# Attention probabilities turned by the vector engine and by transfers within SBUF, in place of the tensor engine

## The chip, the core and the metric

The kernel runs on one core of a Trainium2 chip. The metric is the device time of one execution in microseconds (us); lower is better.

The engines are named as in the profile: PE is TensorE (PEld its weight loads), DVE VectorE, ACT ScalarE, POOL GpSimd, SP SyncE, whose queue (SPq) here issues every DMA of the program.

## What is computed

Cross-attention with low-rank additions to the weights, in float32, for 8 batches of 256 queries and 256 context rows of width 1024, with 32 query heads and 8 key/value heads of 32 columns:

```python
q = _lora_linear(hidden_states, Wq, Aq, Bq)      # (8, 256, 1024), 32 heads
k = _lora_linear(traces, Wk, Ak, Bk)             # (8, 256, 256), 8 heads, each used by 4 query heads
v = _lora_linear(traces, Wv, Av, Bv)
scores = einsum('bhqd,bhtd->bhqt', q, k) / sqrt(32)
attn = softmax(scores, axis=-1)
context = einsum('bhqt,bhtd->bhqd', attn, v)
return hidden_states + _lora_linear(context, Wo, Ao, Bo)
```

## The kernel before

A prologue folds the low-rank products into the weights (`fold_mms`) and projects batch 0. Then a loop runs over seven batches (`Fori(0, NB - 1)` on each engine), the last batch is written out after it, and the output projection follows for all batches (`out_batch`).

Every projection operand is split into a high and a low part, so a product is three matmuls. A projection group is 24 matmuls of 256 columns (`group_step`, L858), and a batch has 12 groups (`BODY`).

A batch is 32 **slots**. A slot m works on two heads for 128 queries; four slots make a **unit**, one key/value head with its four query heads. In slot s, each engine does this, in the order written:

- PE (`slot`, L952): `turn` (L893) transposes the probabilities of slot s, four 128x128 transposes through the identity into a PSUM bank; `scores` (L878) makes the scores of slot s + 4, two matmuls; then 9 matmuls of the projection groups (L868). In the first slot of each unit it adds `context` (L901) of the unit before: 8 float32 matmuls, each 128 rows by 32 columns of stationary data with 256 moving columns.
- DVE: copies the turned block from PSUM to `probs_t` in three slots of four (L263), takes the row maxima for slot s + 4 (`row_max`, L718), the reciprocals (L750), evicts the low part of a projection (L712), and copies the context to `ctx_stage` once a unit (L764). The low part of x is made at L725.
- ACT: copies the turned block in the fourth slot (L263), and computes the exponentials (L582), after the turn of slot s has been made, because the buffer `probs` holds four slots.
- POOL: multiplies the probabilities by the reciprocals (`normalize`, L525), 3 slots ahead.

SP is a queue that is worked in order. Projected q and k parts go to DRAM (`send_q`, L305, `send_k`, L310) and come back as three DMAs each (`stack_q`, L293, `stack_k`, L315), in the layout that the scores matmul wants. `wait` (L268) waits for a semaphore before the DMAs that stand behind it, and nothing behind a wait is issued before it ends. The list of one batch is written out by hand in `body` (L362): 4 + 4 input loads, 8 times `stack_q` (24 DMAs), 8 `send_q`, 2 `send_k`, 2 `stack_k` (6 DMAs) and 8 `store_ctx` (L369), 56 DMAs in all.

Of the kernel before, what the change touches and what calls it, by code (L numbers as in the profile page):

```python
# [27 lines left out]
P = 128  # L28
NB = 8
S = 256  # L30
# [12 lines left out]
FIRST = 3  # L43
GROUP_MM = 3 * KT
FILL = 9
DMA = 16
# [11 lines left out]
BODY = [("q", 4, 0), ("q", 5, 0), ("k", 0, 1), ("q", 6, 0), ("q", 7, 0), ("k", 1, 1),  # L58
# [13 lines left out]
V1_EARLY, V1_SLOT = 16, 4  # L72
# [3 lines left out]
def xattn(nc, xt, ct, xn, wq, wkv, wo, a4, b4kv, b4q, b4o, out):  # L76
    with ExitStack() as ctx:
# [18 lines left out]
        v_sb = sb("v_sb", [P, 2, KV], F32)  # L96
        probs = sb("probs", [P, 4, 2, S], F32)
        probs_t = sb("probs_t", [P, 2, 2, GH, S], F32)
# [7 lines left out]
        w_sum = sb("w_sum", [P, 2, 512], F32)  # L106


        probs_flat = probs[:].rearrange("p a b c -> p (a b c)")
        pt_flat = probs_t[:].rearrange("p a b c d -> p (a b c d)")  # L110
# [19 lines left out]
        turn_bank = [banks[:, 4 + i, :] for i in range(2)]  # L130
# [46 lines left out]
        pt_dve = sem("pt_dve")  # L177
        pt_act = sem("pt_act")
# [16 lines left out]
        def end_slot(i):  # L195

            return FIRST + (GROUP_MM * (i + 1) - 1) // FILL

# [50 lines left out]
        def fold_chunks(s):  # L249

            early = (16, 17, 19, 20, 21, 23, 24, 25)
# [4 lines left out]
        def turn_of(unit, c):  # L256

            return turn_bank[(5 * unit + (0, 2, 3, 4)[c]) % 2]

        def copy_turned(op, unit, c):  # L260
            dst = probs_t[:, unit % 2, :, 2 * (c % 2):2 * (c % 2) + 2, P * (c // 2):P * (c // 2 + 1)]
            src = turn_of(unit, c).rearrange("p (t h q) -> p t h q", t=2, h=2)
            return op(dst, src, ACT.Copy) if op == nc.scalar.activation else op(dst, src)  # L263


        @block.sync
        def _(sp):
# [41 lines left out]

            def send_k(m, count):  # L310
# [42 lines left out]
            for g in range(4):  # L353
# [3 lines left out]
            stack_q(2, 2, 4)  # L357

# [3 lines left out]
            def body(b, last):  # L362
# [16 lines left out]

                pos = {g: i for i, g in enumerate(LAST if last else BODY)}  # L380
                for j in range(4):
# [8 lines left out]
                stack_q(3, fills + 2, score0 + 8)  # L390
                store_ctx(0)
                send(pos["q", 4, 0])
                stack_q(4, fills + 3, score0 + 12)
                send(pos["q", 5, 0])
                store_ctx(1)
                for j in range(4):
                    wait(c_ready, b * 4 + (j + 5))
                    if not last:
                        load_inputs(xt, b + 1, j)
                    else:  # L400
                        load_w(FOLD_O + j)
                stack_q(5, fills + 3, score0 + 16)
                if not last:
                    send(pos["k", 0, 1])
                    stack_k(0, b + 2, score0 + 16)
                store_ctx(2)
                send(pos["q", 6, 0])
                stack_q(6, fills + 4, score0 + 20)
                if last:
                    send(pos["q", 7, 0])  # L410

                    for g, loads in ((3, 2), (None, 2), (4, 1), (5, 3), (6, 2), (7, 2)):
                        for _ in range(loads):
                            load_w(next(late_w))
                        if g is None:
                            stack_q(7, fills + 4, score0 + 24)
                        else:
                            store_ctx(g)
                        if g == 6:
                            wait(ctx_mm, NB * NG - 1)  # L420
                            for i in range(2):
                                wait(ctx_stored[i], DMA * (1 + 2 * NG // 2))
                            load_ctx(1, 1)
# [661 lines left out]
```

## Time and profile before

| | |
|---|---|
| time, median of 3 runs (lowest to highest) | 756.04 us (756.01 to 756.3) |
| span of the profiled execution, first to last instruction | 753.1 us |
| granted TensorE clock, mean | 0.998 |
| PE busy | 737.6 us, 98% of the span |
| weight loads busy | 645.2 us, 86% |
| DVE busy | 469.0 us, 62% |
| ACT busy | 382.0 us, 51% |
| POOL busy | 349.1 us, 46% |
| DMA moved | 117.01 MB, mean 155 GB/s |

The profile is of one execution. Its instructions span 753.1 us; the 2.9 us up to the median lie before the first and after the last of them. The busy time of PE comes from modelled ends of pipelined matmuls, so it tells when PE had work and not how fast it was. Issuing a DMA is not counted as busy time of any engine; the issues are rows of SPq in the timeline.

### The profile page before, as it was taken

Reading aid. Unit: us, or ns where it says so; the run is one execution under the profiler, and the core shown is the slowest. Engines: PE = TensorE matmul, PEld = TensorE weight load, DVE = VectorE, ACT = ScalarE, POOL = GpSimd, SP = SyncE. Lnnn points to the kernel's source line nnn. Section 1 sums busy time; section 2 is a strip of 40 time slices with the busy share of each in tenths; the row PEclk is TensorE's granted clock in tenths of the full one; section 3 lists DMA queues with packets and bytes.
Section 4 is the critical chain, followed back from the end, with each engine's and each line's share of the span. In section 5 each row is a group of like instructions: output and inputs, shape, how many; then the busy total and the mean of one; then the engine's idle time right before and its main releaser. Section 6 shows DMA issues by size and latency. Waiting matters only on the chain.

```text
span 753.1 us, 17856 instructions
## 1 busy us (share of the span) xinstructions
PE 737.6 (98%) x5776; PEld 645.2 (86%) x5776; DVE 469.0 (62%) x988; ACT 382.0 (51%) x1287; POOL 349.1 (46%) x322
## 2 busy tenths in 40 slices
PE   7899999999999999999999999999999999999998
PEld 6678899889989989999998998999867788888886
DVE  5957687687768668767876866787696412212211
ACT  4437665666666666666666666665685210111100
POOL 4757645745654574565557457555766100000000
PEclk9999999999999999999999999999999999999999
DMA  7775544554453555345454544645464834343331
GB/s 257 271 219 164 169 140 140 159 172 122 139 174 126 157 152 163 119 139 175 138 156 149 155 131 128 172 139 178 139 181 154 276 130 156 117 167 111 111 111 56
DMA packets 94665, 117.01 MB, mean 155 GB/s; under 512 B 8624, under 2 KB 76208, under 8 KB 94640
## 3 DMA queue, kind: packets, MB, share of 16 engines
q1 hardware_dynamic: 94640, 116.69, 49.3%
q8 instruction: 14, 0.23, 0.1%
q14 instruction: 11, 0.09, 0.0%
HBM read 78.91 MB, written 37.75 MB: 155 GB/s over the span
## 4 chain that ended last, share of the span: by engine, by line
PE 88%; DVE 5%; DMA 2%; issue 2%; POOL 1%; ACT 0%; SPq 0%; POOLq 0%; DVEq 0%
PE banks L868 32%; PE banks L917 23%; PE banks L897 15%; PE banks L906 8%; PE banks L882 7%; DVE neg_max L718 2%; PE banks L853 2%; DVE x_lo L725 2%; DMA probs_t<-wq 1%; PE banks L855 1%; DMA probs<-b4q 1%; DMA probs_t<-b4kv 1%; POOL k_stack L510 1%; DVE lora L679 0%; DVE probs_t L263 0%
## 5 line engine op out<-in xcount | busy, mean ns | idle before, releaser
L525 POOL TENSOR_TENSOR probs<-probs,rsums 128x512 f32<-128x512 f32 x256 | 266.4, 1041 | 205.4 <-DVE rsums L750 204.6
L582 ACT ACTIVATE probs<-banks,neg_max 128x256 f32<-128x256 f32 x512 | 238.7, 475 | 175.7 <-DVE neg_max L718 170.8
L718 DVE TENSOR_REDUCE neg_max<-banks 128x2 f32<-128x512 f32 x256 | 174.3, 682 | 20.0 <-PE banks L882 20.0
L897 PE MATMUL banks<-ident,probs 128*128 128x128 f32 x1024 | 157.1, 276 | 2.2 <-POOL probs L525 2.0
L263 DVE COPY probs_t<-banks 128x512 f32<-128x512 f32 x192 | 132.4, 690 | 43.0 <-PE banks L897 35.6
L868 PE MATMUL banks<-x_hi,w_hi 128*128 128x256 f32 x512 | 145.7, 285 | 0.8 <-POOL w_lo L500 0.4
L868 PE MATMUL banks<-x_hi,w_lo 128*128 128x256 f32 x512 | 144.6, 282 | 0.0
L868 PE MATMUL banks<-x_lo,w_hi 128*128 128x256 f32 x512 | 144.5, 282 | 0.0
L897 PEld LDWEIGHTS banks<-ident,probs 128*128 128x128 f32 x1024 | 115.5, 140 | 30.8 <-issue 27.1
L882 PE MATMUL banks<-k_stack,q_stack 96*128 96x256 f32 x512 | 122.8, 322 | 0.0
L582 ACT ACTIVATION_READ_ACCUMULATOR probs<-banks,neg_max 128x1 f32 x512 | 104.0, 203 | 0.0
L868 PEld LDWEIGHTS banks<-x_hi,w_hi 128*128 128x128 f32 x512 | 97.2, 190 | 2.2 <-DVE x_lo L725 1.6
L868 PEld LDWEIGHTS banks<-x_lo,w_hi 128*128 128x128 f32 x512 | 98.0, 191 | 0.0
L868 PEld LDWEIGHTS banks<-x_hi,w_lo 128*128 128x128 f32 x512 | 97.8, 191 | 0.0
L819 DVE TENSOR_TENSOR raw<-banks,probs 128x512 f32<-128x512 f32 x32 | 21.4, 689 | 118.4 <-PE banks L917 116.7
L882 PEld LDWEIGHTS banks<-k_stack,q_stack 96*128 96x128 f32 x512 | 77.1, 191 | 0.3 <-DMA q_stack<-q_parts 0.3
L906 PE MATMUL banks<-probs_t,v_sb 128*32 128x256 f32 x1024 | 68.5, 385 | 0.0
L764 DVE COPY ctx_stage<-banks 128x256 f32<-128x256 f32 x64 | 27.1, 424 | 55.5 <-PE banks L906 55.5
L917 PE MATMUL banks<-w_hi,c_hi 128*128 128x512 f32 x128 | 49.9, 390 | 0.5 <-POOL w_lo L500 0.5
L917 PE MATMUL banks<-w_lo,c_hi 128*128 128x512 f32 x128 | 49.9, 390 | 0.0
L917 PE MATMUL banks<-w_hi,c_lo 128*128 128x512 f32 x128 | 49.8, 389 | 0.0
L917 PE MATMUL banks<-w_hi,x_hi 128*128 128x512 f32 x128 | 49.8, 389 | 0.0
(76 smaller groups left out, 1112.9 us busy)
## 6 DMA issues: line engine op xcount, KB each, us to landing
q_stack<-q_parts SPq DMA_DIRECT2D x192, 128.0 KB, 2.5
q_parts<-q_stage SPq DMA_DIRECT2D x64, 256.0 KB, 2.2
raw<-ct SPq DMA_DIRECT2D x32, 256.0 KB, 3.9
raw<-xt SPq DMA_DIRECT2D x32, 256.0 KB, 4.4
context<-ctx_stage SPq DMA_DIRECT2D x64, 128.0 KB, 1.8
probs<-xn SPq DMA_DIRECT2D x16, 512.0 KB, 4.1
out<-raw SPq DMA_DIRECT2D x15, 512.0 KB, 2.9
probs_t<-context SPq DMA_DIRECT2D x7, 1024.0 KB, 5.9
```

What stands on the lines that cost most here:

```text
L263: return op(dst, src, ACT.Copy) if op == nc.scalar.activation else op(dst, src)
L525: nc.gpsimd.tensor_tensor(probs[:, c], probs[:, c], rsums[:, c, :].unsqueeze(2).broadcast_to([P, 2, S]), ALU.mult).then_inc(norm_done, 1)
L582: last = nc.scalar.activation(probs[:, c, h, :], score_bank[c][:, S * h:S * (h + 1)], ACT.Exp, bias=neg_max[:, c, h:h + 1], scale=-1.0, ac ...
L718: nc.vector.tensor_reduce(out=neg_max[:, c, :], in_=score_bank[c].rearrange("p (h t) -> p h t", h=2), axis=AXIS, op=ALU.min).then_inc(max_ ...
L725: nc.vector.tensor_tensor(cols[1], raw[:, j, :], cols[0], ALU.subtract).then_inc(ready, 1)
L764: nc.vector.tensor_copy(ctx_stage[:, u % 2, :], turn_bank[(5 * unit + 1) % 2][:, 0:S]).then_inc(ctx_done, 1)
L819: nc.vector.tensor_tensor(out_rows[h][:, cols], banks[:, 4 * i + 2 * h + half, :], x_rows[h][:, cols], ALU.add).then_inc(o_out, 1)
L868: mm = nc.tensor.matmul(proj_bank[bank][:, 0:S], lhs, rhs, start=(k == 0), stop=(k == GROUP_MM - 1))
L882: last = nc.tensor.matmul(score_bank[c][:, S * h:S * (h + 1)], q_stack[0:3 * HD, g % 2, head, P * qh:P * (qh + 1)], k_stack[0:3 * HD, g, : ...
L897: last = nc.tensor.transpose(bank[:, P * (2 * t + h):P * (2 * t + h + 1)], probs[:, c, h, P * t:P * (t + 1)], ident[:])
L906: last = nc.tensor.matmul(bank[HD * h:HD * (h + 1), 0:S], v_sb[:, t, HD * (unit % NG):HD * (unit % NG + 1)], probs_t[:, unit % 2, t, h, :] ...
L917: mm = nc.tensor.matmul(banks[:, 4 * i + 2 * qh + half, :], o_parts[i][t_part][:, kt, P * qh:P * (qh + 1)], w_hl[w_part][:, kt, 512 * half ...
```

## The change

The transposes on PE go. DVE turns the probabilities in blocks of 32x32, SBUF to SBUF, once a slot, into a new tile `turned_in`. Such a turn leaves the context rows spread over the wrong groups of 32 partitions, so that for each unit SP issues 8 DMAs of 32 partitions by 1024 float32 (128 KB each) from `turned_in` to `probs_t`. The copies from PSUM to `probs_t` on DVE and ACT go. The context matmul is cut into 64x32 tiles with 128 moving columns, 32 matmuls in place of 8, over two PSUM banks, and runs two units behind (`LAG = 8` slots) where it ran one slot behind its unit. The v parts are written as two half copies, and two DMAs a batch duplicate them into the other half of the partitions.

With this, FIRST (where the projection groups start in a batch) goes from slot 3 to 5, the order of groups changes (q6 and q7 ahead of k0), two projection groups of the prologue move into its first slots, and `w_sum` shares the memory of `q_stage`.

```diff
+        def turned_out(unit, c):
+            return turned_in[:, unit % 2, :, :, c].rearrange("p e k h q -> p h k e q")
...
+            def move_turned(b, unit, ctxs):
+                wait(turned, b * SLOTS + 4 * unit + 4)
+                if ctxs is not None:
+                    wait(ctx_mm, ctxs)
+                i = unit % 2
+                for half in range(2):
+                    for f in range(2):
+                        for e in range(2):
+                            row, to = 64 * half + 32 * f, 64 * half + 32 * e
+                            sp.dma_start(probs_t[to:to + 32, i, f],
+                                         turned_in[row:row + 32, i, e]).then_inc(pt_moved[i], DMA)
+
+            def copy_v(evicted):
+                wait(proj_out, evicted)
+                for half in range(2):
+                    tiles = v_rep[:].rearrange("p (m k) n -> p k m n", k=2)[:, half]
+                    sp.dma_start(tiles[64 * (1 - half):64 * (2 - half)],
+                                 tiles[64 * half:64 * (half + 1)]).then_inc(v_moved, DMA)
...
+            def turn(n, i, reuse):
+                dve.wait_ge(norm_done, n + (i + 1))
+                if reuse is not None:
+                    dve.wait_ge(pt_moved[(i // 4) % 2], reuse)
+                nc.vector.transpose(turned_out(i // 4, i % 4),
+                                    probs[:, i % 4].rearrange("p h t -> p (h t)")).then_inc(turned, 1)
...
+            def context(b, unit):
+                pe.wait_ge(pt_moved[unit % 2], (b * 4 + (unit // 2 + 1)) * (DMA * MOVES))
+                if unit == 0:
+                    pe.wait_ge(v_moved, b * (2 * DMA) + 2 * DMA)
+                else:
+                    pe.wait_ge(ctx_done, b * NG + unit)
+                pe.sem_inc(pe_waits, 1)
+                for k in range(4):
                     for h in range(GH):
...
+                        for half in range(2):
+                            rows = slice(64 * half, 64 * (half + 1))
+                            moving = probs_t[rows, unit % 2].rearrange("p f k (a c) h q -> p k c h a f q", a=2)
+                            last = nc.tensor.matmul(
+                                ctx_bank[half][HD * h:HD * (h + 1), 0:P],
+                                v_rep[rows, k, HD * unit:HD * (unit + 1)], moving[:, k, h // 2, h % 2],
+                                start=(k == 0), stop=(k == 3), tile_position=(64 * half, HD * h))
```

The list of SP in a batch of the loop becomes: `copy_v`, 4 loads, stack q3, **move 1**, send q4, store 0, stack q4, **move 2**, send q5, 2 loads, store 1, stack q5, send q6, 2 loads, **move 3**, stack q6, store 2, send q7, **move 4**, stack q7, store 3, send k0, **move 5**, stack k0, send k1, send q0, store 4, stack q0, **move 6**, send q1, store 5, stack q1, stack k1, send q2, **move 7**, stack q2, send q3, store 6, **move 0** of the next batch, store 7. (k and q from k0 on are those of the next batch.)

On SP, where the second half of a batch begins. L307 and L310 store q, L312 and L336 store k, L299 and L302 stack q, L320 and L344 stack k, L371 and L397 store the context. Before:

```order
L307 DMA q_parts<-q_stage 128x2x256 [waits proj_out]
L271 REGISTER_ALU [waits q_stored1]
L299 DMA q_stack<-q_parts 32x4x256 [waits scores_mm]
L299 DMA q_stack<-q_parts 32x4x256 x2
L271 REGISTER_ALU
L312 DMA k_parts<-k_stage 128x2x256 [waits proj_out]
L271 REGISTER_ALU
L371 ISA [waits ctx_done]
L371 DMA context<-ctx_stage 128x256
```

and now:

```order
L323 DMA probs_t<-turned_in 32x1024 [waits turned,ctx_mm]
L323 DMA probs_t<-turned_in 32x1024 x7
L274 REGISTER_ALU [waits q_stored1]
L302 DMA q_stack<-q_parts 32x4x256 [waits scores_mm]
L302 DMA q_stack<-q_parts 32x4x256 x2
L274 REGISTER_ALU
L397 ISA [waits ctx_done]
L397 DMA context<-ctx_stage 128x256
L274 REGISTER_ALU
L336 DMA k_parts<-k_stage 128x2x256 [waits proj_out]
```

Eight DMAs more stand in the queue for each unit, between a q store and the stacking of its parts. A batch has 122 DMAs now, 64 of them moves and 2 for v.

On PE, at the first slot of a unit, where the context is made. Before:

```order
L868 MATMUL banks<-x_hi,w_lo 128x256
L1010 REGISTER_ALU
L906 MATMUL banks<-probs_t,v_sb 32x256 [waits pt_dve,pt_act]
L906 MATMUL banks<-probs_t,v_sb 32x256 x7
L956 REGISTER_ALU
L960 REGISTER_ALU [waits norm_done]
L897 MATMUL banks<-ident,probs 128x128 [waits pt_dve]
L897 MATMUL banks<-ident,probs 128x128 x3
L882 MATMUL banks<-k_stack,q_stack 128x256 x2
```

and now:

```order
L957 ISA
L959 REGISTER_ALU [waits pt_moved0]
L968 MATMUL banks<-probs_t,v_rep 32x128 [waits v_moved]
L968 MATMUL banks<-probs_t,v_rep 32x128 x31
L951 ISA
L1026 REGISTER_ALU [waits q_stacked1]
L944 MATMUL banks<-k_stack,q_stack 128x256 [waits exp_done]
L944 MATMUL banks<-k_stack,q_stack 128x256
L930 MATMUL banks<-x_hi,w_hi 128x256
```

The four transposes of the slot are gone, the context has four times as many matmuls, and it waits for the moves' landing.

On DVE, one slot in the middle of a batch. Before:

```order
L263 COPY probs_t<-banks 128x2x2x128 [waits turned]
L717 REGISTER_ALU
L718 TENSOR_REDUCE neg_max<-banks 128x2 [waits scores_mm]
L750 RECIPROCAL rsums<-sums 128x2 [waits exp_done]
```

and now, in the first slot of a unit:

```order
L806 ISA [waits norm_done]
L807 STREAM_TRANSPOSE turned_in<-probs 128x2x4x2x32 [waits pt_moved0]
L767 REGISTER_ALU
L768 TENSOR_REDUCE neg_max<-banks 128x2 [waits scores_mm]
L800 RECIPROCAL rsums<-sums 128x2 [waits exp_done]
```

The transpose takes the place of the copy and stands in every slot; it waits for the normalized probabilities, and once a unit for the moves that read the buffer it writes.

## Rows read from the trace of the kernel before

**Rows 1.** The page: busy time of PE, and the chain that ended last by engine

```profile
PE 737.6 (98%) x5776; PEld 645.2 (86%) x5776; DVE 469.0 (62%) x988; ACT 382.0 (51%) x1287; POOL 349.1 (46%) x322
...
PE 88%; DVE 5%; DMA 2%; issue 2%; POOL 1%; ACT 0%; SPq 0%; POOLq 0%; DVEq 0%
```

**Rows 2.** Stretches: their length; busy us of each engine; clock, DMA share, GB/s

```profile
0.00:20.00 20.00, 15.28 (x84) 14.10 (x85) 10.71 (x13) 8.21 (x13) 9.11 (x12) 0.91 0.77 267
98.00:163.50 65.50, 65.47 (x610) 59.50 (x610) 48.56 (x113) 42.37 (x155) 38.20 (x36) 1.00 0.50 154
523.00:586.00 63.00, 61.97 (x474) 47.91 (x472) 46.53 (x103) 42.71 (x137) 42.97 (x39) 1.00 0.53 161
586.00:753.00 167.00, 163.48 (x720) 135.06 (x720) 37.77 (x40) 12.18 (x7) 0.23 (x1) 1.00 0.40 139
```

**Rows 3.** The chain in order of time: the same step in two batches

```profile
164.38 1.17 DVE x_lo L725
...
229.93 1.17 DVE x_lo L725
```

**Rows 4.** Timeline of PE, a slot and a context: start us, us, engine, line

```profile
303.91 0.60 PE L897 MATMUL banks<-ident,probs 128*128 128x128 f32 x4
304.27 0.48 PE L882 MATMUL banks<-k_stack,q_stack 96*128 96x256 f32 x2
304.58 0.28 PE L868 MATMUL banks<-x_hi,w_hi 128*128 128x256 f32 x1
...
305.55 0.28 PE L868 MATMUL banks<-x_hi,w_lo 128*128 128x256 f32 x1
305.75 1.07 PE L906 MATMUL banks<-probs_t,v_sb 128*32 128x256 f32 x16
306.76 0.33 PE L897 MATMUL banks<-ident,probs 128*128 128x128 f32 x1
```

**Rows 5.** Timeline of SP's queue where it hardly waits, 276 to 293 us

```profile
276.28 0.38 SPq L307 DMA_DIRECT2D q_parts<-q_stage  x1
276.99 0.37 SPq L371 DMA_DIRECT2D context<-ctx_stage  x1
277.60 2.07 SPq L277 DMA_DIRECT2D raw<-xt  x4
279.93 1.28 SPq L299 DMA_DIRECT2D q_stack<-q_parts  x3
281.39 0.38 SPq L312 DMA_DIRECT2D k_parts<-k_stage  x1
```

**Rows 6.** The three DMAs of one stack_q there, one by one

```profile
279.93 0.33 SPq L299 DMA_DIRECT2D q_stack<-q_parts  x1
...
280.31 0.42 SPq L299 DMA_DIRECT2D q_stack<-q_parts  x1
...
280.78 0.43 SPq L299 DMA_DIRECT2D q_stack<-q_parts  x1
```

**Rows 7.** Waits of SP's queue: us in total, times, longest us

```profile
SPq L273 <- DMA q_parts<-q_stage: 60.4, 35, 1.9
```

**Rows 8.** Line L299: issue durations, ns min/median/max, first and last start

```profile
L299 SPq DMA_DIRECT2D q_stack<-q_parts x192: 303/424/1172, 51.2 to 557.9; - x192
```

**Rows 9.** DMA issues: KB each, median us to landing

```profile
q_stack<-q_parts SPq DMA_DIRECT2D x192, 128.0 KB, 2.5
q_parts<-q_stage SPq DMA_DIRECT2D x64, 256.0 KB, 2.2
...
context<-ctx_stage SPq DMA_DIRECT2D x64, 128.0 KB, 1.8
```

**Rows 10.** Groups of DVE instructions: busy us, mean ns; and one timeline row

```profile
L263 DVE COPY probs_t<-banks 128x512 f32<-128x512 f32 x192 | 132.4, 690 | 43.0 <-PE banks L897 35.6
...
L725 DVE TENSOR_TENSOR x_lo<-raw,x_hi 128x512 fp32r<-128x512 f32 x32 | 26.3, 830 | 0.0
...
228.66 0.68 DVE L725 TENSOR_TENSOR x_lo<-raw,x_hi 128x512 fp32r<-128x512 f32 x1
```

More of the change, by code:

```diff
@@ L42 @@
 NORM_AHEAD = 3
-FIRST = 3
+FIRST = 5
 GROUP_MM = 3 * KT
 FILL = 9
+LAG = 8
 DMA = 16
@@ L352, in _ @@
                 stack_k(m, 1, None)
-            for g in range(4):
+            for g in range(3):
                 send_q(g, g + PRO_Q + 1)
@@ L390, in body @@
                 stack_q(3, fills + 2, score0 + 8)
+                move_turned(b, 1, None)
+                send(pos["q", 4, 0])
                 store_ctx(0)
-                send(pos["q", 4, 0])
                 stack_q(4, fills + 3, score0 + 12)
+                move_turned(b, 2, unit0 + 1)
                 send(pos["q", 5, 0])
+                load_x(0)
+                load_x(1)
                 store_ctx(1)
[L396 to L401, printed above, removed]
@@ L409, in body @@
                 if last:
[L410 to L423, printed above, removed]
+                    load_w(next(late_w))
@@ new lines, in body @@
+                    load_w(next(late_w))
+                    load_w(next(late_w))
+                    store_ctx(5)
+                    load_w(next(late_w))
+                    move_turned(b, 7, unit0 + 6)
+                    load_w(next(late_w))
+                    load_w(next(late_w))
+                    store_ctx(6)
+                    wait(pt_moved[0], DMA * MOVES * NB * NG // 2)
+                    for i in range(2):
+                        wait(ctx_stored[i], DMA * (1 + 2 * NG // 2))
@@ L452, in _ @@
                 load_rows(0, h)
-            wait(ctx_mm, NB * NG)
+            wait(pt_moved[1], DMA * MOVES * NB * NG // 2)
             load_ctx(2, 0)
@@ L608, in _ @@
                     high(c_hl, 2 + f, c_hi_done, 1)
-            for g in range(4):
+            for g in range(3):
                 if g == 2:
@@ L637, in slot @@
                         w_high(f)
-                if not prologue and s in (4, 5):
-                    for j in (2 * (s - 4), 2 * (s - 4) + 1):
+                if prologue and s == 3:
+                    proj_high("q", 3, (3 + PRO_Q) % 2, 3 + PRO_Q, DMA)
+                if not prologue and s in (6, 7):
+                    for j in (2 * (s - 6), 2 * (s - 6) + 1):
                         act.wait_ge(proj_mm, b * PER + PRO)
@@ L743, in _ @@
                     proj_low("v", 0, 0, PRO_Q - 1, None, None)
-            for g in range(4):
+            for g in range(3):
                 if g == 2:
@@ L798, in _ @@
                     slot(b, s, False)
-            for s in range(FIRST, SLOTS + 2):
+            for s in range(FIRST, SLOTS + LAG - 3):
                 slot(NB - 1, s, True)
@@ L950, in _ @@
                     group_step(kind, i, j % 2, k)
+            stacks_ready(0, 0)
+            for m in range(4):
+                scores(m, 0, m)
             def slot(b, s, last, prologue=False):
```

185 lines of the change are left out of this document (98 added, 87 removed).

## The prediction

> **What bounds the kernel now.** I read the page first: PE is busy for 98% of the span, and the chain that ended last runs through PE for 88% of it [rows 1]. The stretches say where [rows 2]: a batch of the loop (65.5 us) keeps PE busy for 65.47 us at full granted clock (2.4 GHz), with DVE at 48.56, ACT at 42.37, POOL at 38.20 us and the DMA engines at a share of 0.50. The same step of the chain returns after 229.93 - 164.38 = 65.55 us [rows 3], which I take as the period of a batch; seven batches run so. The last batch takes some 63 us, the output projection 167 us [rows 2], and that one the change leaves alone.
>
> The timeline of PE shows what the period is made of [rows 4]. A slot starts at 303.91 with the transposes, at 304.27 come the scores, at 304.58 the nine projection matmuls. So four transposes cost 0.36 us of PE and two scores 0.31 us. Nine projection matmuls take 1.09 us: the last starts at 305.55 and takes 0.12 like the others' distance, to 305.67. The context then lasts until the next transposes at 306.76, 1.09 us. A unit is 4 x 1.75 + 1.09 = 8.1 us, eight make 65 us: PE fills the period by itself.
>
> The busy table has no row for SP, so its queue has to be read from the timeline [rows 5]. There the queue hardly waits, and the distance from start to start is what each thing costs it, waits and registers included: a load 0.58 us (four in 279.93 - 277.60), a stack of three DMAs 1.46 us, a q store 0.71 us ahead of a context store and about 0.56 otherwise, a context store 0.61. Within a stack the DMAs start 0.38 and then 0.47 us apart [rows 6]. For a batch: 8 loads 4.7 us, 10 stacks 15 us, 10 q and k stores 6 us, 8 context stores 4.8 us, in sum 30.5 us. SP issues for under half of the period and waits for the rest; that is why no chain goes through it now (SPq 0% [rows 1]).
>
> **The change, part by part, for one batch.**
>
> *Transposes off PE.* 32 slots x 0.36 us = 11.5 us less. PE would need 32 x 1.39 + 8 contexts of 1.09 = 53.2 us.
>
> *Context in 32 matmuls.* The 16 records of today (8 float32 matmuls, two each) become 64 of half the columns, on half the rows. Lower bound: twice as many tiles beside each other keep the array time, 1.09 us. Upper bound: no overlap, at the 0.09 us from one transposition of 128 columns to the next [rows 4], 64 x 0.09 = 5.8 us. Today's context has 256 columns at 1.07/16 = 0.07 us a record, so it does overlap. I take 1.5 us, near the low end; PE then needs 56.5 us. Up to 2.8 us, 67 us a batch, it changes nothing below.
>
> *DVE.* 24 copies of 0.69 us go, 32 transposes of the same 128x512 come. At the copy's 0.69 us [rows 10] DVE goes from 48.6 to 54 us. The upper bound is another op of that size with both ends in SBUF, x_lo: 0.68 us in one row, 830 ns in the mean, 1.17 in the chain [rows 3, 10]; at 1.17 DVE would have 69 us. A transpose reads one tensor where x_lo reads two, so I take 0.69: hidden. ACT loses 8 copies, POOL keeps its work, and both have room.
>
> *Moves.* 64 DMAs a batch on SP, the one queue. Nothing in the trace moves 32 partitions within SBUF, but what a DMA costs the queue hardly depends on what it carries: single ones of 256 KB (q store) and 128 KB (context store) take 0.38 and 0.37 us [rows 5, 9]. In a run the first takes 0.33 us, the next 0.42 to 0.43 us with 0.05 between [rows 6]. Eight in a row: 0.38 + 7 x 0.475 + 0.15 for the wait = 3.85 us; eight units, 30.8 us. Lower bound, if each went at the first one's 0.38: 25.5 us. Upper bound: issues that are held up, of which 1.17 us is the longest [rows 8], up to 40 us. I take 30.8, because the second and third of each stack are the same situation.
>
> *v.* Two DMAs and a wait, 1.0 us. The loop's branch adds 0.4.
>
> *SP's sum*: 30.5 + 30.8 + 1.0 + 0.4 = **62.7 us of issuing in a batch**, where PE needs 56.5. SP becomes the bound, at 96% of today's period, even if it never waits.
>
> *It does wait.* Stack q4 needs q4's store to have landed; 35 such waits took 60.4 us, 1.7 us each [rows 7], with nothing between store and stack. In the new list a context store (0.6 us) alone stands between them for q4, q0 and q1, so 1.1 us is left each time, 3.3 us a batch; the others have a move or two loads in between. Everything behind is held, the next move too. That gives 66.0 us. The DMA engines are also fuller: 267 GB/s at a share of 0.77 is 347 GB/s at full load [rows 2], the moves carry 64 x 131 KB = 8.4 MB, 24 us, and the share goes from 0.50 to (32.8 + 24.2)/67 = 0.85. Issues and landings stretch then; I put 1.3 us a batch on it (nothing to 6 us), two or three issues like the long one of rows 8. **Period 67.3 us**, 1.75 more than now, 12.3 us over seven batches.
>
> *PE* idles for over 10 us in each batch, in gaps of a microsecond or two before scores and contexts. In all loop stretches the granted clock is 1.00 [rows 2]; I put no cost on it.
>
> *Last batch.* SP has fewer stacks and stores here: seven moves 27 us, five stacks 7.5, the rest (two v, 4 + 16 loads, 4 + 8 stores, the first context load) about 17, with two of the waits 54 us. PE's 62 us lose 29 transposes of a slot (10.4 us) and gain 8 x 0.4. Both leave some 56 us of 63: 7 us saved.
>
> *Prologue.* The move of group 0 (3.85 us) stands ahead of the first batch's loads; most of it is covered by the slots that run then. I put 2 us (0 to 5).
>
> Sum: 756.0 + 12.3 - 7 + 2 = **763.3 us** (span 753.1 + 7.3 = 760.4; the 2.9 us outside the span stay). The median of the runs is the base, and the rows sum to its span.
>
> **A rule against the trace.** The first and third lines of rows 9 carry 128 KB each: the q stack, onto 32 partitions, lands after 2.5 us, the context store, out of 128 partitions, after 1.8. The Trainium skill, SBUF — State Buffer, section "Door 1: The DMA port swizzle", says that 32 partitions reach 8 of the 16 SBUF ports, so half the rate. The trace does not settle it, since the two also differ in direction and place in the queue. By the rule a move would run at half rate; that is the third rival below.
>
> **Rivals.**
>
> 1. *SP is no bound (faster).* The place is the eight DMAs of a move. If they start every 0.38 us or less, as the first of a stack does, SP's sum is 30.5 + 25.5 + 1.4 + 3.3 = 60.7 us, and with the landing waits hidden it is 57. Then PE's 56.5 us, DVE's 54 and their mutual waits set a period near 60. Time: 756 - 7 x 5.5 - 9 + 2 = 710 us. It decides below a distance of 0.45 us from move to move. For it: the first DMAs of all runs are that cheap. Against it: no second one in rows 6 is. A milder form has 0.475 us but all landing waits and stretching gone: 62.7 us, 756 - 20 - 7 + 2 = 731 us. Together 0.28.
>
> 2. *The context is not overlapped (slower).* At 5.8 us a context PE has 44.5 + 8 x 5.8 = 91 us a batch, some 940 us in all; it bites from 2.8 us on. At 4 us it is 76.5 us and 833 us. Against it: 16 records in 1.07 us now. 0.06. DVE at 1.17 us a transpose belongs beside it: 69 us a batch, about 780 us, 0.05.
>
> 3. *The moves are slow in the DMA engines (slower).* If 8.4 MB take twice the 24 us, the engines have 32.8 + 48.4 = 81 us of work in a batch: 756 + 7 x 15.6 = 865 us. Between full and half rate it begins to bind at 34 us. For it: each move reads and writes the same 64 partitions. Against it: stacks onto 32 partitions land only 0.7 us later. 0.11.
>
> That the change doesn't do what it says is excluded by the order of instructions: no transposition is left on PE in the loop.
>
> **How the numbers follow.** Forecast 0.50: SP bound, period 66 to 71 us, 757 to 790 us, likeliest 763. Rival 1 0.28, rivals 2 and 3 with DVE's 0.22. Within 0.2%, 1.5 us and about what a measurement of this kernel can tell from no change, lies a narrow strip between rival 1's mild form and the forecast: 0.05. Faster: 0.28, and 0.03 from a cheaper last batch, so 0.31. Slower: 0.64. The range goes down into rival 1 (its 731, not its 710) and up into a half-bitten rival 3: 722 to 812 leaves out about 0.2.
>
> **What would show it.** Right: SPq rows of L323 8 in a row, 0.42 to 0.43 us each, with almost no idle time in SP's queue over a batch; a same step of the chain returning after 66 to 69 us; SPq or the moves in the chain; PE busy share down to 80 to 88%, idle before scores and context with q_stack or probs_t as releaser; DMA share near 0.85. Wrong: L323 issues of 0.35 us or a period under 62 us (rival 1); context rows of 3 us and more with PE still at 98% (rival 2); moves landing after 5 us and more with a share at 0.95 (rival 3); a DVE transpose of over 1 us.

## The result and the profile after

| | before | after |
|---|---|---|
| median of the runs, us | 756.02 (755.58 to 756.3) | 957.69 (954.66 to 962.48) |
| span of the profiled execution, us | 753.1 | 955.8 |
| granted clock, mean | 0.998 | 0.858 |

The ratio is 1.2675, with a 95% interval of 1.2638 to 1.2712. I had said slower, by 7 us, with 722 to 812 as the range; it is slower by 202 us. Of two kernels further down (1091.05 and 766.91 us) one execution each lay over 1.5% above the kernel's fastest; without it the medians are 1087.92 and 766.05 us, and the ratios given leave it out.

Where the 202.7 us of span came in can be read from the first load of ct in each batch. It stands (in the last batch the load of the context in its place) at 61.5 us before and 76.6 after: 15.1 us ahead of the loop. Seven batches then take 65.66 us each before and 90.06 after: 170.8 us. From there to the end it is 232.0 us before and 248.8 after: 16.8 us. So this is a story of the loop. The timeline of SP's queue shows its length, as the distance of the v copies of two batches one after another, 439.50 - 347.40 = 92.1 us (the longest of the seven):

```profile
347.40 1.36 SPq L331 DMA_DIRECT2D v_rep<-v_rep  x2
...
439.50 1.36 SPq L331 DMA_DIRECT2D v_rep<-v_rep  x2
```

The page of the changed kernel: busy time, the instruction queue (packets, MB, share), and the chain that ended last:

```profile
PE 715.4 (75%) x7824; PEld 639.5 (67%) x7824; DVE 502.4 (53%) x1068; ACT 361.3 (38%) x1223; POOL 348.8 (36%) x322
...
q8 instruction: 72, 1.18, 0.5%
...
issue 42%; POOL 26%; PE 19%; DMA 5%; DVE 4%; SPq 2%; POOLq 1%; ACT 1%; DVEq 0%; ACTq 0%
```

Against [rows 1] PE has fallen from 98% to 75% and no engine is full. SPq has 2% of the chain, which would acquit SP if read alone. But "issue" has 42%: stretches in which the chain, which here runs back along POOL's normalizations, found nothing that released it. In the longest piece near 410 us, PE stood still for most of it and waited for a q stack, as its timeline shows below:

```profile
406.60 1.04 POOL probs L577
407.64 6.25 issue
```

The windows answer to [rows 2], with a middle stretch of two batches and then the last batch and the output projection:

```profile
98.00:163.50 65.50, 44.83 (x645) 42.26 (x644) 39.63 (x93) 28.54 (x107) 24.95 (x24) 0.84 0.83 212
300.00:480.00 180.00, 124.67 (x1720) 117.46 (x1713) 105.72 (x245) 79.74 (x292) 76.33 (x72) 0.81 0.80 206
...
705.70:794.60 88.90, 63.06 (x740) 48.21 (x739) 45.15 (x97) 37.44 (x115) 39.23 (x36) 0.85 0.79 203
800.00:955.00 155.00, 152.60 (x674) 126.02 (x672) 34.24 (x37) 11.51 (x6) 0.00 (x0) 1.00 0.40 142
```

The output projection is as it was. In the middle stretch the clock is at 0.81 and PE busy for 69%. Who stops PE and DVE stands in the groups (busy us, mean ns, then idle before and its releaser):

```profile
L944 PE MATMUL banks<-k_stack,q_stack 96*128 96x256 f32 x512 | 128.2, 339 | 176.4 <-DMA q_stack<-q_parts 163.1
...
L807 DVE STREAM_TRANSPOSE turned_in<-probs 128x512 f32<-128x512 f32 x256 | 178.8, 699 | 55.7 <-DMA probs_t<-turned_in 52.8
...
L968 PE MATMUL banks<-probs_t,v_rep 64*32 64x128 f32 x4096 | 76.2, 278 | 43.7 <-DMA probs_t<-turned_in 29.5
```

Two things of the forecast stand here: a DVE transpose takes 0.70 us, and the context's records are short. But the largest wait, 163.1 us, is for the stacks of q, which the change does not touch: they come late. SP's timeline over one unit:

```profile
408.49 1.27 SPq L302 DMA_DIRECT2D q_stack<-q_parts  x3
409.94 4.96 SPq L323 DMA_DIRECT2D probs_t<-turned_in  x8
415.09 1.30 SPq L310 DMA_DIRECT2D q_parts<-q_stage  x1
416.73 0.38 SPq L397 DMA_DIRECT2D context<-ctx_stage  x1
418.47 1.26 SPq L302 DMA_DIRECT2D q_stack<-q_parts  x3
```

The eight moves take 4.96 us, 5.15 with the step to the next DMA, where I had taken 3.85 with such a step, and the store behind them, 0.38 us in [rows 5], takes 1.30. Line L323 by itself (ns min/median/max) has a median of 592, against 424 of the stacks in [rows 8]:

```profile
L323 SPq DMA_DIRECT2D probs_t<-turned_in x512: 507/592/2345, 69.0 to 777.4; - x171
```

PE meanwhile, over the same unit (columns: start us, us, engine, line; in brackets the idle time before):

```profile
404.16 0.28 PE L930 MATMUL banks<-x_hi,w_lo 128*128 128x256 f32 x1
...
405.30 1.15 PE L968 MATMUL banks<-probs_t,v_rep 64*32 64x128 f32 x64 [0.87 <-DMA probs_t<-turned_in]
412.25 0.79 PE L944 MATMUL banks<-k_stack,q_stack 96*128 96x256 f32 x2 [5.80 <-DMA q_stack<-q_parts]
412.84 0.41 PE L930 MATMUL banks<-x_hi,w_hi 128*128 128x256 f32 x1
413.06 0.41 PE L930 MATMUL banks<-x_lo,w_hi 128*128 128x256 f32 x1
```

The context of 64 records takes 1.15 us. Then PE stands for 5.80 us until a q stack is there, and behind that gap the projection matmuls start 0.21 us apart, where they started 0.12 apart in [rows 4]: the granted clock from 409.0 to 414.0 us is 0.50, the lower of its two levels.

Why that stack came late can be followed back. Its three DMAs were issued from 408.49 on, when the store of its q had landed. The store had begun at 405.54, though DVE had the low part of that q ready at 401.16; the last two of eight moves, a k stack and a k store stood ahead of it. The next q, ready at 406.84, had to wait until 415.09, behind the stack and the moves in the rows above:

```profile
400.75 0.41 DVE L762 TENSOR_TENSOR q_stage<-banks,q_stage 128x256 fp32r<-128x256 f32 x1
...
406.44 0.40 DVE L762 TENSOR_TENSOR q_stage<-banks,q_stage 128x256 fp32r<-128x256 f32 x1
```

Over five batches a q store begins 4.5 us after its q is ready, where it was 0.7 us before. Landings have grown too, against [rows 9] (last column, us from issue to landing):

```profile
probs_t<-turned_in SPq DMA_DIRECT2D x512, 128.0 KB, 3.5
q_stack<-q_parts SPq DMA_DIRECT2D x192, 128.0 KB, 4.1
q_parts<-q_stage SPq DMA_DIRECT2D x64, 256.0 KB, 2.6
```

### The profile page after: what moved, and what is told of

Read it like the earlier page. It is cut to its first block, busy times and chain, and to the rows that moved or that the text cites. A ratio compares the mean times of both kernels' runs of the same rounds, so it can differ in the third digit from the quotient of the medians.

```text
span 955.8 us, 22470 instructions
## 1 busy us (share of the span) xinstructions
PE 715.4 (75%) x7824; PEld 639.5 (67%) x7824; DVE 502.4 (53%) x1068; ACT 361.3 (38%) x1223; POOL 348.8 (36%) x322
## 4 chain that ended last, share of the span: by engine, by line
issue 42%; POOL 26%; PE 19%; DMA 5%; DVE 4%; SPq 2%; POOLq 1%; ACT 1%; DVEq 0%; ACTq 0%
POOL probs L577 22%; PE banks L978 17%; POOL c_lo L548 3%; SPq L323 1%; DMA raw<-wo 1%; DMA q_stack<-q_parts 1%; DMA probs_t<-turned_in 1%; DVE turned_in L807 1%; DVE neg_max L768 1%; PE banks L930 1%; DVE lora L728 1%; POOLq L576 1%; DMA probs<-b4q 1%; DMA q_parts<-q_stage 1%; DMA turned_in<-wq 1%
## 5 line engine op out<-in xcount | busy, mean ns | idle before, releaser
L944 PE MATMUL banks<-k_stack,q_stack 96*128 96x256 f32 x512 | 128.2, 339 | 176.4 <-DMA q_stack<-q_parts 163.1
L944 PEld LDWEIGHTS banks<-k_stack,q_stack 96*128 96x128 f32 x512 | 96.2, 230 | 197.2 <-issue 177.6
L807 DVE STREAM_TRANSPOSE turned_in<-probs 128x512 f32<-128x512 f32 x256 | 178.8, 699 | 55.7 <-DMA probs_t<-turned_in 52.8
L930 PE MATMUL banks<-x_hi,w_hi 128*128 128x256 f32 x512 | 161.5, 315 | 1.0 <-POOL w_lo L552 0.8
L930 PEld LDWEIGHTS banks<-x_hi,w_hi 128*128 128x128 f32 x512 | 115.4, 225 | 1.6 <-issue 0.9
L930 PEld LDWEIGHTS banks<-x_lo,w_hi 128*128 128x128 f32 x512 | 115.1, 225 | 0.0
L930 PEld LDWEIGHTS banks<-x_hi,w_lo 128*128 128x128 f32 x512 | 113.9, 222 | 0.0
L968 PE MATMUL banks<-probs_t,v_rep 64*32 64x128 f32 x4096 | 76.2, 278 | 43.7 <-DMA probs_t<-turned_in 29.5
L968 PEld LDWEIGHTS banks<-probs_t,v_rep 64*32 64x32 f32 x4096 | 59.1, 107 | 54.3 <-issue 50.3
L548 POOL TENSOR_TENSOR c_lo<-raw,c_hi 128x512 fp32r<-128x512 f32 x32 | 40.8, 1274 | 36.3 <-ACT c_hi L605 36.3
L978 PE MATMUL banks<-w_hi,x_lo 128*128 128x512 f32 x128 | 49.8, 389 | 0.0
```

What stands on the lines that cost most here:

```text
L548: nc.gpsimd.tensor_tensor(cols[1], raw[:, j, :], cols[0], ALU.subtract).then_inc(c_ready, 1)
L807: nc.vector.transpose(turned_out(i // 4, i % 4), probs[:, i % 4].rearrange("p h t -> p (h t)")).then_inc(turned, 1)
L930: mm = nc.tensor.matmul(proj_bank[bank][:, 0:S], lhs, rhs, start=(k == 0), stop=(k == GROUP_MM - 1))
L944: last = nc.tensor.matmul(score_bank[c][:, S * h:S * (h + 1)], q_stack[0:3 * HD, g % 2, head, P * qh:P * (qh + 1)], k_stack[0:3 * HD, g, : ...
L968: last = nc.tensor.matmul(ctx_bank[half][HD * h:HD * (h + 1), 0:P], v_rep[rows, k, HD * unit:HD * (unit + 1)], moving[:, k, h // 2, h % 2] ...
L978: mm = nc.tensor.matmul(banks[:, 4 * i + 2 * qh + half, :], o_parts[i][t_part][:, kt, P * qh:P * (qh + 1)], w_hl[w_part][:, kt, 512 * half ...
```

## The experiments

Four theories stood for the missing 195 us. **P**: the moves of 32 partitions crowd a part of the DMA paths. **B**: their bytes. **Q**: the number of their issues on SP's queue. **O** or **L**: the order of SP's list and the latencies from a q store to its scores. A fifth, **I**, came up on the way. Each run's median stands against that of the kernel before on the same chip (755.4 to 756.9 us).

**The halves in turn** (upper and lower partitions alternate)

```
-                for half in range(2):
-                    for f in range(2):
-                        for e in range(2):
+                for f in range(2):
+                    for e in range(2):
+                        for half in range(2):
```

> The same eight moves of a unit, in an order that alternates between partitions 0-63 and 64-127 in place of four of one half and then four of the other. The 4 KB packets of the moves took 285 ns in the mean where those of the loads took 159, and a move's issue took 0.67 us where I had 0.43. Theory P (the ends of a move lie on half of the SBUF ports, and four such moves in a row queue on the same half): two neighbours now run beside each other, issues go back towards 0.43 us, the period of a batch from 90 us to 70-75 us, the time to 810-840 us. Theory B (the DMA engines are slow for these bytes whatever the ports): nothing changes, 940-970 us.

955.51 us, against 957.69 of the change: the same. **The moves over 128 partitions**, eight of 1 KB a partition (the blocks are not exchanged):

```
+                for f in range(2):
+                    for k in range(4):
+                        sp.dma_start(probs_t[:, i, f, k], turned_in[:, i, f, k])
```

> Eight moves of the same 128 KB per unit, but each over all 128 partitions with rows of 1 KB, to the same partition that they came from (so the data of the context is wrongly arranged). Count and bytes as in the changed kernel, all ports reached. Theory P: issues 0.43 us, period 66-70 us, 770-800 us. Theory B: as in the changed kernel, over 900 us. If SP's order and waits alone made the period, also over 900 us with short issues.

947.02 us, 1% less than the change. **A quarter of the bytes**, `probs_t[to:to + 32, i, f, 0]` from `turned_in[row:row + 32, i, e, 0]`:

> The eight moves of a unit as in the changed kernel, 32 partitions each, but a quarter of each row (1 KB of 4 KB), so three quarters of the probabilities are not moved. The count stays, the bytes go from 8.4 to 2.1 MB a batch. My forecast's sum (issues of 0.43 us, period 67 us) should hold here: 765-790 us. If issues were slow because of the count or the shape of the moves, they stay at 0.67 us and the time over 900 us.

933.68 us, with the DMA share down from 0.80 to 0.47. My forecast's sum, which was to hold here (765 to 790 us), did not. An issue still takes what it took: line L324 there is the moves', a quarter of the size.

```profile
L324 SPq DMA_DIRECT2D probs_t<-turned_in x512: 507/591/1926, 68.7 to 755.2; - x171
```

P falls: none of these runs comes near its 770 to 840 us. Three quarters of the bytes are worth 24 us.

**One transfer a unit**, first a tiny one, then one with all bytes over 128 partitions (`probs_t[:, i]` from `turned_in[:, i]`); MOVES = 1 in both:

> One tiny move per unit in place of eight (probabilities are not moved at all; only the order of waits is kept). Neither count nor bytes. SP then issues some 35 us in a batch, PE needs 53-57 us: period 56-62 us, 680-730 us. This is what the change could have given if the moves cost nothing. Should it stay near 765 us, the moves are not what limits it.

> One transfer a unit over all 128 partitions carries all 1 MB that the eight carried, from its place to the same place (so the blocks aren't exchanged and the output is not the reference's). Against the one small transfer a unit (794.9 us) this adds the bytes alone. Theory Q (the number of issues on SP): within 1.5% of that run, 790 to 806 us, with SP's queue still idle for a third of the time. Theory B (bytes through the DMA engines, which the changed kernel moves at 285 ns a 4 KB packet): most of the 160 us between 794.9 and 957.7 comes back, 880 us or more.

The tiny one: 794.87 us, a ratio of 1.0509 (1.0462 to 1.0557), where I had expected 680 to 730. The full one: 863.19 us, between the ranges of the two theories. So from 794.9 the bytes alone, in one transfer of 1 MB a unit, add 68 us, the issues alone (quarter of the bytes, 933.7) up to 139, both together 163. The bytes cost more where the queue is not full: B holds for a part. And without any real move the rest of the change is still slower than before.

**The issues put into the kernel before.** Behind each context store, eight more transfers of 64 bytes on 32 partitions, within SBUF or to DRAM:

```
+                    wait(extra_done, (unit0 + g) * (EXTRA * DMA) + DMA)
+                    for e in range(EXTRA):
+                        sp.dma_start(extra_dst[:, e], extra_src[:]).then_inc(extra_done, DMA)
```

> The kernel before, with eight more transfers of 64 bytes on 32 partitions behind each store of a context, from one place of SBUF to another; nothing waits for them but the next eight. It measures the price of the issues on SP's queue with everything else of the kernel before in place. SP issued for 30.5 us in a batch of 65.55 us. Theory Q: 64 more at 0.63 us start to start are 40 us, 71 us of issuing and more with its waits, so SP becomes the bound: a period of 74 to 84 us, 825 to 900 us in all. Theory O (the order of SP's list and the lag of the context are what costs, and the issues fit beside): 756 to 775 us.

> As the run with eight more transfers inside SBUF, but they go from SBUF to DRAM. If the issue of a transfer with one end in DRAM costs 0.33 us first and 0.43 after, as the stacks and loads of the kernel before show, 64 more are 28 us, SP issues for 58 us of 65.55, and the time is 756 to 790 us, clearly under the run inside SBUF. If an issue costs the same wherever the transfer goes (what I took for the prediction), both runs give the same time within 1%.

> The run with eight more transfers inside SBUF, with four instead: 32 a batch, 20 us of issuing, 51 us with the 30.5 that were there, in a batch of 65.55. Theory Q in its plain form (the issues cost nothing until SP's queue is full): 756 to 765 us. Theory L (each issue ahead of a send or a stack also delays the chain of q and k, which has little slack): 775 to 850 us, about half of what eight cost.

Within SBUF 940.27 us, ratio 1.2427 (1.2381 to 1.2473); to DRAM 857.08, 1.1302 (1.1233 to 1.1371); four within SBUF 801.67, 1.062 (1.0589 to 1.065). One of the first kernel's eights, one of the second's, and the lines in the whole of each:

```profile
416.64 4.96 SPq L381 DMA_DIRECT2D extra_dst<-extra_src  x8
...
L381 SPq DMA_DIRECT2D extra_dst<-extra_src x512: 507/590/1426, 73.4 to 767.1; - x171
```

```profile
415.88 3.57 SPq L381 DMA_DIRECT2D extra_dst<-extra_src  x8
...
L381 SPq DMA_DIRECT2D extra_dst<-extra_src x512: 312/421/1673, 74.2 to 690.5; - x171
```

The first is the run that settles most. 2 KB each, nothing else changed, and the kernel before is nearly as slow as the change, slower even than Q's 900. An issue within SBUF costs 590 ns, to DRAM 421: the two kernels with eight differ in nothing else and lie 83 us apart, though the second is over its 790 too. Q holds, but not in its plain form: with four, the queue is not full, and the batch is 5.5 us longer all the same (71.1 against 65.6 us). The waits of PE there are for the stacks of q.

The queue can be read as in the forecast, from start to start, over five batches from the third on. A gap of over 0.25 us between two instructions of SP counts as a wait, all other time as occupied; the last column is the time from the end of the eviction of a q to the start of its store:

| kernel | batch, us | SP occupied | SP waits | q ready to its store, us |
|---|---|---|---|---|
| before | 65.5 | 31.8 | 33.7 | 0.7 |
| before, four more within SBUF | 70.4 | 53.8 | 16.6 | 3.3 |
| before, eight more to DRAM | 77.4 | 62.4 | 14.9 | 4.9 |
| before, eight more within SBUF | 87.9 | 74.1 | 13.9 | 7.6 |
| change, one tiny move a unit | 71.0 | 43.5 | 27.5 | 1.0 |
| change | 90.2 | 82.8 | 7.4 | 4.5 |

In the kernel before with more issues, the stores start later and the batch grows while SP still waits for 14 to 17 us of it: the price comes through the chain of q. In the change SP is occupied for 92% of a batch, so there Q holds too. The change with one tiny move has neither a full queue nor late stores; its 39 us come from something else.

**Half of the moves on ACT's queue**, behind the exponentials of a unit's last slot:

```
-                for half in range(2):
+                for half in range(1):
...
+                    for f in range(2):
+                        for e in range(2):
+                            act.dma_start(probs_t[64 + 32 * e:96 + 32 * e, i, f],
+                                          turned_in[64 + 32 * f:96 + 32 * f, i, e])
```

> The changed kernel with the four moves of the upper 64 partitions issued on ACT's queue, behind the exponentials of the group's last slot, and the other four on SP's; the same bytes, the same packets, the output the reference's. Theory Q (SP's queue is occupied for 93% of a batch and sets its 90 us): 32 issues of 0.62 us a batch leave SP, 20 us, and the period falls to 68 to 80 us, 790 to 880 us in all; ACT, busy 45 us of a batch, can take 20 more. Theory B (the bytes of the moves through the DMA engines): 935 to 960 us, as the eight narrow transfers of the changed kernel.

911.08 us, ratio 1.2029 (1.198 to 1.2078): neither. SP's issues add up to 17.6 us less a batch, the batch is 6.7 shorter, and SP now waits for 19.8 us of it. ACT pays 0.62 us for each issue in front of its next exponentials, and the bytes stay: a q store lands after 3.9 us, 2.6 in the change.

```profile
L691 ACTq DMA_DIRECT2D probs_t<-turned_in x256: 514/616/2347, 68.5 to 731.7; - x128
...
q_parts<-q_stage SPq DMA_DIRECT2D x64, 256.0 KB, 3.9
```

**No moves needed.** In the order of the kernel before, DVE turns straight into probs_t, and the context takes each block of 32 queries where it lies, in tiles of 32 rows (`tile_position=(32 * g, HD * h)`, 128 matmuls of 64 columns a unit), V copied to all four groups of partitions. Then the same with the context of the change, 32 matmuls a unit, on data that is not in place.

> The kernel before in its order and with its FIRST of 3, where DVE turns the 32x32 blocks straight into probs_t and nothing is moved: the context multiplies each block of 32 queries where it lies, in tiles of 32 rows by 32 columns (128 matmuls of 64 columns a unit in two halves), and V is copied to the other three groups of partitions by six transfers a batch. The output is the reference's. PE loses 32 x 0.36 = 11.5 us of transposes in 65.55 us and pays 8 times (context 1.2 to 2.3 less 1.09 us): 55 to 64 us a batch; DVE has about 55 us of work a batch as in the changed kernel. Theory Q (with the moves gone, turning by DVE pays): a period of 57 to 64 us, 690 to 745 us in all, faster than before. Theory O (turning by DVE doesn't pay whatever moves or not, because DVE or the chain of the q stacks ends last): 760 us or more.

> The run with 32 rows a tile, whose context is put back to the 32 matmuls of 64 rows and 128 columns of the changed kernel, on probabilities and copies of V that no transfer has put in their place (so the context is not the reference's); no moves at all, SP's list and FIRST as in the kernel before. If the 256 short matmul records a unit are what made that run 1091 us (PE sat without instructions in the second half of a context, gaps of 1.3 to 3.6 us), this gives a period of 54 to 60 us, DVE's 55 us being the bound, and 670 to 720 us: what the change could have won had the moves cost nothing. If DVE's or the stacks' chain is the cause there, it stays over 756 us.

1091.05 us for the first, far over what I expected. Its PE timeline at one context:

```profile
426.76 1.48 PE L928 MATMUL banks<-probs_t,v_rep 32*32 32x64 f32 x128
428.17 0.50 PE L896 MATMUL banks<-k_stack,q_stack 96*128 96x256 f32 x2
428.60 0.77 PE L928 MATMUL banks<-probs_t,v_rep 32*32 32x64 f32 x55
431.59 0.97 PE L928 MATMUL banks<-probs_t,v_rep 32*32 32x64 f32 x73 [2.22 <-issue]
```

The first 128 records take 1.48 us; in the second half PE runs nothing for 2.22 us, and the profile shows nothing that it waits for. There are 73 such gaps ahead of context records, 1.8 us in the mean and 4.0 at most. Its page counts 168 packets in the instruction queue. The second version takes 809.28 us: slower than before, though SP's list is the old one but for six copies of v, no moves are left, and DVE has 51 us of work in its 72 us batch. Its contexts run later than in the kernel before. Between the two versions only the form of the context differs, so 256 short records a unit in place of 64 cost some 280 us.

**What the long issues are.** The changed kernel has issues of 0.95 to 2.1 us on SP, nine a batch. One suspect was a setting that came with it, `dynamic_dma_scratch_size=1024`, alone in the kernel before:

> The kernel before with the program's scratch for dynamic transfers cut to 1024 bytes, as the changed kernel has it, and nothing else. The changed kernel and all its relatives show issues of 0.95 to 2.1 us on SP's queue (some 45 between 90 and 500 us), the kernel before one. If the scratch is their cause, they appear here and the time is 1 to 6% longer; if not (the longer program, or the transfers inside SBUF), 755 to 758 us and the stacks' issues stay at 0.33 and 0.43 us.

757.5 us, ratio 1.0006 (0.9985 to 1.0028): not that. The trace's packet list had the answer: the change reads 16 KB packets of instructions at 402.53, 415.07, 426.34, 432.81 and 436.05 us, and its long issues start at 402.71, 415.09, 426.30, 432.78 and 436.01. The kernel before reads no such packet between 119 and 525 us. Theory I follows: PE's loop has become longer than what is held, and is read again in each batch. Three tests: the kernel before with its context matmuls cut in three (columns 0 to 128, to 192, to 256), and two kernels with `for k in range(2)` in place of `range(4)` in the context, the version without moves and the change.

> The kernel before with each matmul of the context cut into three, of 128, 64 and 64 columns: the same work, and 7824 matmul records in place of 5776, as many as the changed kernel has. The output is the reference's. Between 119 and 525 us the kernel before reads no packet of its instruction queue (14 in all), the changed kernel one of 16 KB about every 10 us (72 in all), and its issues of 1.1 to 2.1 us on SP's queue stand at the same moments. Theory I (a loop body longer than what the chip holds is read again in every batch, and the reading stalls PE and SP): some 70 packets here too, long issues on SP's queue, and 765 to 810 us. If the packets come from something else of the change: 14 packets and 755 to 762 us.

> The run without moves, with half of the context's matmuls left out (two of the four tiles of keys), so 5776 records of matmuls as in the kernel before; half of the context is not computed. Theory I: 14 packets of instructions, the gaps in which PE waited for nothing in the profile go, and the period falls from about 68 us to 54 to 60, 680 to 730 us in all. Theory L (what holds the run without moves is the chain of loads, splits, projections and stacks, whose latencies are longer than the 55 us of work): 785 to 810 us still.

> The changed kernel with half of the context's matmuls left out (two of the four tiles of keys; 5776 records of matmuls), its moves untouched. Theory I for its share: about nine long issues a batch go, 0.8 us each, and PE's stalls with them; SP stays occupied: a period of 80 to 86 us, 880 to 930 us. If the packets of instructions don't matter beside the moves: 945 to 960 us.

| kernel | matmul records | instruction packets | us | mean batch, us | issues over 0.75 us in five batches |
|---|---|---|---|---|---|
| before | 5776 | 14 | 756.0 | 65.66 | 0 |
| before, context cut | 7824 | 72 | 775.53 | 68.31 | 8 |
| change | 7824 | 72 | 957.69 | 90.06 | 45 |
| change, half the context | 5776 | 14 | 915.2 | 83.63 | 0 |
| no moves | 7824 | 72 | 809.28 | 71.96 | 14 |
| no moves, half the context | 5776 | 14 | 766.91 | 65.33 | 0 |
| eight more within SBUF | 5776 | 14 | 940.27 | 89.13 | 0 |

In all three pairs the packets come and go with the number of matmuls, and the long issues with them. What the packets hold is not in the trace; that it is PE's loop is inferred from this. The kernel with half a context and no moves met neither of its ranges: 14 packets as theory I has it, but 766.91 us and not 680 to 730 (ratio 1.012, 1.0065 to 1.0175). The page of the cut kernel, its stack issues, and a stop of PE between two projection matmuls and the transposes:

```profile
q8 instruction: 72, 1.18, 0.7%
...
L299 SPq DMA_DIRECT2D q_stack<-q_parts x192: 303/424/1664, 54.3 to 580.5; - x192
...
339.94 1.05 PE L897 MATMUL banks<-ident,probs 128*128 128x128 f32 x4 [1.93 <-POOL probs L525]
```

Ratio 1.0258 (1.023 to 1.0286). That PE stop has POOL as its releaser, though a packet of instructions was read from 336.81 us on; which of the two it was I can't tell from the row. The pairs give 20, 42 and 42 us. In the first the cut itself costs PE next to nothing, a context taking 1.02 us in the median against 1.00. In the last two half of the context's work is gone as well, 8 x 0.6 us of PE a batch at most, so 42 is an upper bound. In the change without half of its context, the moves' line has the same median and no issue of 2 us:

```profile
L323 SPq DMA_DIRECT2D probs_t<-turned_in x512: 507/591/1783, 69.7 to 734.9; - x171
```

The version without moves and with half a context still takes 65.3 us a batch, with PE busy for 53 and DVE for 50 of it. No queue is full and nothing is read again. What is left would be theory L, the time from a q projection through a store, a stack and their two landings to its scores; this is argued and not shown, since no run shortened that chain by itself.

## Why the prediction was wrong

**PE as the bound now, and PE's work after it** held, at the upper level of the clock. A context takes 1.15 us (I took 1.5), so rival 2 had no part.

**DVE** held: 0.70 us a transpose, 0.69 taken.

**Moves, 64 at 0.475 us**: this step failed first. I had argued that a DMA's cost to the queue hardly depends on what it carries, which is true (2 KB and 128 KB alike take 590 ns), and took the second and third DMA of a stack as "the same situation". They are not: they have an end in DRAM. Eight moves occupy the queue for 5.15 us (409.94 to 415.09) and not 3.85: 41.2 us a batch in place of 30.8, above the 40 that I had kept as the upper bound. With the long issues among them they occupy it for 47.3 us.

**SP's other issuing, 30.5 us**: 31.8 by the same count in the kernel before, 33.5 in the change. Nine issues a batch, 38 of 45 of them moves, stood beside an instruction read, and the change itself brought these reads by its longer program. I counted the 64 records of a context as PE time and never as instructions. Price: at most 6.4 us a batch.

**SP's sum of 62.7 us, and 3.3 and 1.3 us for waits and stretching**: the mechanism was right in the change, since SP is occupied for 92% of the period, and the size was not. The sum is 82.8 us, 20.1 more: 16.5 in the moves, 1.0 in the v copies, 2.6 in the rest. The waits are 7.4 us. Together they are the period of 90.2 us, where I had 67.3.

**The sum on SP against PE's sum**, as a rule, failed as well. I let the larger of two sums set the period. The run with four more issues shows that a queue occupied for 53.8 us of 70.4 already costs 5.5 us a batch. Eight more within SBUF, with none of the change's other parts, give 87.9 us where SP is occupied for 74.1. Issues ahead of a q store delay the scores behind it: it starts 3.3 and 7.6 us after its q is ready there, and 4.5 in the change, against 0.7. With 41.2 us for the moves and all else as I had it, my own sum would have given 77.7 us a batch, an estimate of 836 us in all: most of the way to the runs is still missing.

**Landings and bytes**: underrated. The share of 0.85 that I forecast is 0.80, but over 90 us. The kernel before needs 0.50 x 65.6 = 33 us of the engines, the change 0.80 x 90 = 72, so 8.4 MB of moves cost 39 us and not 24.2, which is nearer rival 3's 48.4. The Trainium skill, SBUF — State Buffer, section "Door 1: The DMA port swizzle", gives a transfer on 32 partitions half the ports. The trace agrees in direction: a move lands after 3.5 us in the median, and after 2.6 where the same bytes go over 128 partitions. But it does not set the period: that run takes 947 us. Rival 3 was nearer to the rate than I was, and had the bound wrong. Three quarters of the bytes are worth 24 us on top of the issues, all of them 68 by themselves.

**"I put no cost on it"**, said of the clock, failed. PE's waits for a q stack are 3.9 us in the mean and 9.0 at most, not one or two, and behind them matmuls run 0.21 us apart. PE is busy for 124.67 / 180 x 90.06 = 62.4 us a batch where I took 56.5. For 20.8 us of a batch it is busy at the lower level; at the upper one the same work takes no less than half, so the clock costs 10.4 us a batch at most. How much of that the waits hide was not measured.

**Last batch, 7 us saved; prologue, 2 us lost**: 16.8 lost from the last batch on, for which no run has the cause, and 15.1 ahead of the loop. With one tiny move a unit the first load of ct in the loop still stands at 74.3 us, 12.8 later than before, so the moves are 2 us of the 15.1.

The direction was right, and that SP's queue decides. That a queue near its limit costs only what it exceeds was wrong. By the runs the 202 us split into about 163 for the moves (957.7 against 794.9) and 39 for the rest of the change, and somewhere in both lie the instruction reads, up to 42 us in the whole. What makes up the 39 beside these reads stays open: FIRST at 5, the order of SP's list, the later contexts and the turning on DVE were not separated. The version with the old list and no moves, at 809 us, shows that the old list by itself does not bring the time back.

## What to carry to other kernels

Price an issue by a row of the same kind: both ends, not only the size. When work moves from an engine to a queue, don't only compare sums; list what stands behind each new entry in the queue and how much slack it has until its consumer, because a chain of a store, a stack and two landings in a queue in order starts to pay before the queue is full. And count instructions, not only time: with a third more matmul records this program went from no instruction packet in the middle of its loop to nine a batch.

## What was unexpected of the hardware

- A DMA within SBUF on 32 partitions costs SP's queue 590 ns (ACT's 616), one with an end in DRAM 421 to 424, whether 2 KB or 128 KB; over 128 partitions it is 601 within SBUF, and the v copies on 64 take 648. The shortest take 507 and 303 to 312.
- With 5776 matmul records the program has 14 packets in its instruction queue, with 7824 it has 72 and with 20112 it has 168, of 16 KB each; the kernel cut to 7824 records with the same work is 20 us slower. In the change 45 of them and 45 issues of over 0.75 us on SP fell into five batches; the ten between 390 and 490 us that I compared each start within 0.5 us of one another.
- 128 matmul records on tiles of 32 rows, 64 columns each, run in 1.48 us, but with two such blocks a unit PE stands for up to 4.0 us within or ahead of one, with no wait in the profile. Why was not tested.
- Two levels of TensorE's clock show in one timeline: 0.12 us from matmul to matmul before a gap of 5.8 us at a granted clock of 1.00, 0.21 behind it at 0.50.
